# A two-direction Mamba-2 block with a feed-forward layer: all instruction orders drawn anew, a transpose of 64 columns in place of 32, and an unread negation taken out

## Chip, cores and metric

One core of a Trainium2 chip. The metric is the device time of one execution in microseconds (us), the median of several runs.

## What is computed

Eight sequences of 512 tokens, 256 wide, all float32. Each is layer-normed and goes through two Mamba-2 blocks, one forward in time and one backward (d = 0 and d = 1 below); their outputs are projected and added to the input, then comes a second layer norm and a linear layer with a low-rank correction.

```python
zxbcdt = x @ Win                       # 256 -> 2*512 + 2*64 + 8
z, xBC, dt = split(zxbcdt)
xBC = silu(causal_conv4(xBC) + convb)
xs, Bm, Cm = split(xBC)                # 8 heads of 64, state of 64
dt = softplus(dt + dtb); dA = exp(dt * -exp(Alog))
h = dA_t * h + dt_t * B_t x_t;  y_t = C_t h          # over 512 tokens
y = (y + Dsk * xs) * silu(z)
y = y * rsqrt(mean(y*y) + 1e-5) * normw
out_d = y @ Wout
x = x + concat(out_fwd, out_rev) @ Wo + bo
x = x + layernorm(x) @ W.T + b + (layernorm(x) @ V_r) @ C.T
```

## The kernel before

The scan is done in four chunks of 128 tokens, with matmuls inside a chunk and a carried state between chunks. All work of a sequence is cut into steps, and each engine (TensorE `pe`, ScalarE `act`, VectorE `dve`, GpSimd `pool`, and SyncE `sp`, which issues the DMAs) has a list of step calls written out by hand in a fixed order. Semaphores tie the lists together. An engine works its list strictly in order, so a step that waits holds up all that stands behind it on its engine.

The stages in time are `opening` (weights split into a high and a low part, the output weights folded into one, first projections), `first_scan` (sequence 0 forward), then a loop of six passes and the same two lists once more behind it: `reversed_scan` (the backward scan of sequence b, with the projections of sequence b+1 for the forward direction) and `forward_scan` (the forward scan of b+1, with the projections for its backward direction and the second layer norm and feed-forward of sequence b). `last_scan` is the backward scan of the last sequence and the end.

The steps that matter here, with the lines of the profile:

- TensorE. `project(b, d, t)` (L488 to L490): one of nine tiles of 128 output channels, 6 matmuls of 512 columns, into the ring `pj` of three PSUM banks; tile 0 holds B and C, tiles 1 to 4 the values xs, tiles 5 to 8 the gate z. `b_tokens` (L539) and `x_tokens` (L548): transposes of B and xs. `norm_transposed` (L472), `scores` (L555, into `gm`), `squares` (L608), `sums` (L526, L527), `mix` (L622, output projection, a quarter of the tokens each), `norm2_transposed` (L681), `feed` (L688), `dt_project` (L508, L509), `dt_transposed` (L518, 32 rows). `state` (L568) and `intra` (L581) write 64 rows of PSUM with two matmuls side by side; `inter` (L599) uses quarters of 64 by 64; `s_transposed` (L533) transposes the running sums. Everything with `mi` in the profile shares a ring of two PSUM banks; its turns are the lists `START`, `LOOP` and `LAST`.
- ScalarE. `conv_start` (L936) takes a projected tile out of PSUM with the first convolution tap, `conv_end` (L945) applies Silu to the finished tile, `gate` (L950) applies Silu to z. `bound` (L969, Relu, four instructions) and `decay` (L975, Exp) turn the repeated running sums into decay weights, one head each, h = 0 to 7; `decay_w` (L954) and `decay_e` (L959) are Exp on small tiles. `row_copy` (L922) and `row_decays` (L927, Exp) put the transposed sums into the rows that are sent to DRAM and back. `soft_exp` (L914) and `soft_log` (L918, Ln) belong to the softplus. `square` (L989), `norm1_scale` (L998), `norm2_scale` (L1003) and `norm2` (L1008) need no table of their own.
- VectorE. `conv` (L1409, three taps a tile), `weights` (L1436, decay times scores), `x_tokens` (L1421), `state` (L1446, L1448), `outputs` (L1455), `mix` (L1476), `norm2_bn` (L1487), `norm1_aggr` (L1321) and `norm2_aggr` (L1492), `s_copy` (L1383: sums out of PSUM), `s_neg` (L1391: writes `neg_s`, which nothing reads) and `s_rest` (L1397: writes `wd`).
- GpSimd. `decayed_x` (L1907), `decayed_c` (L1913), `decayed_state` (L1921), `gate` (L1928), `add_square` (L1936), and the small steps of the norms (L1852 to L1888).
- SyncE. `put_rows` and `put_decays` write the rows to DRAM, `repeat_heads` (L336) and `repeat_decays` bring them back spread over all partitions, `copy_c` copies C.

x_tokens(j = 0) waits for the four conv_end of its direction, intra(p) for the weights of its two heads, inter(0) for the state of the third chunk on VectorE, mix(0) for all four gated tiles.

```python
            def s_transposed(phase, it, b, d):
                released(phase, it, f"{d}S")
                ps, full = misc(phase, it, f"{d}ST")
                alone(pe)
                pe.transpose(ps[0:NCH, 0:Q], s_all[:, d, 0].rearrange("p c h -> p (c h)"), ident).then_inc(full, 1)
```

NCH is 32, Q is 128; `s_all[:, d]` holds the 32 running sums and then the 32 sums at the chunk ends.

Of the kernel before, what the change touches and what calls it, by code (L numbers as in the profile page):

```python
# [23 lines left out]
ALU = mybir.AluOpType  # L24
ACT = mybir.ActivationFunctionType

P = 128
# [26 lines left out]
START = (["a0", "a1", "dtm", "dtt", "w0", "w1", "w2", "w3", "w4", "0S", "w5", "w6", "0ST", "w7", "w8"]  # L54
         + ["0bt", "0x0", "0x1", "0s0", "0x2", "0x3", "1S", "1ST", "0s1", "0s2"])
LOOP = ["1bt", "1x0", "1x1", "1x2", "1x3", "a0", "a1", "1s0", "1s1", "dtm", "dtt", "0ss", "0o0", "1s2",
        "0o1", "0S", "0ST", "0bt", "0x0", "0x1", "0x2", "0x3", "0s0", "1ss", "0s1", "0s2", "1o0", "1o1",
        "1S", "1ST", "t0", "t1", "f0", "f1", "t2", "t3", "f2", "f3"]
LAST = ["1x0", "1bt", "1x1", "1x2", "1s0", "1x3", "1s1", "0ss", "1s2", "0o0", "0o1", "1o0", "1o1"]
# [15 lines left out]
def build(nc, x, consts, selcol, win, convw, convb, dtb, alog, dskip, normw, woutT, wo, bo, ffT, ffb, vrT, cT, out):  # L75
    with ExitStack() as ctx:
# [57 lines left out]
        neg_s = sb("neg_s", [P, 2, NCH])  # L134
# [45 lines left out]
        def ring(name, n=2):  # L180
# [8 lines left out]
         r_ready, al_ready, s_ready, wd_ready, w_ready, conv_first,  # L189
# [5 lines left out]
            "r_ready al_ready s_ready wd_ready w_ready conv_first bc_ready "  # L195
# [50 lines left out]
        def _(sp):  # L246
# [110 lines left out]
            def opening():  # L357
                load_first(0)
                load_first(1)
                load_first(2)  # L360
                load_first(3)
                load_consts()
                load_small(0)
                load_win(0, 0, 0)
                load_small(1)
                load_win(0, 0, 1)
                load_fold(0)
                load_win(0, 1, 0)
                load_dt()
                load_fold(1)  # L370
                load_fold(2)
                load_win(0, 1, 1)
                load_rest()
# [3 lines left out]
                load_win(1, 1, 1)  # L377
                copy_c(0, 0)
                load_x("start", 0, 1)
                put_rows("start", 0, 0, 0)  # L380
                repeat_heads(0, 0, 0)
                put_decays(0, 0)
                repeat_heads(0, 0, 1)
                repeat_decays(0, 0, 0)
                repeat_decays(0, 0, 1)
                repeat_heads(0, 0, 2)
                repeat_heads(0, 0, 3)
                load_residual0()
                put_rows("start", 0, 0, 1)
                repeat_decays(0, 0, 2)  # L390
                repeat_decays(0, 0, 3)
                repeat_heads(0, 1, 0)
                put_decays(0, 1)
                copy_c(0, 1)
                repeat_decays(0, 1, 0)
                repeat_heads(0, 1, 1)
# [6 lines left out]
            def turn(it, more):  # L403
# [6 lines left out]
                repeat_heads(it + 1, 0, 1)  # L410
                repeat_heads(it + 1, 0, 2)
                repeat_decays(it + 1, 0, 0)
# [5 lines left out]
                store("loop", it, it, 0)  # L418
# [3 lines left out]
                put_decays(it + 1, 1)  # L422
                store("loop", it, it, 1)
                repeat_heads(it + 1, 1, 1)
                repeat_decays(it + 1, 1, 0)
                repeat_decays(it + 1, 1, 1)
                store("loop", it, it, 2)
# [17 lines left out]
        def _(pe):  # L445
# [432 lines left out]
        def _(act):  # L878
# [1269 lines left out]
```

## Time and profile before

| | |
|---|---|
| median of 3 runs | 633.09 us (632.95 to 633.33) |
| the profiled execution: time, span | 633.48 us, 631.6 us |
| mean granted TensorE clock | 0.989 of full speed |
| TensorE matmul busy | 598.1 us |
| ScalarE busy | 551.9 us |
| VectorE busy | 477.6 us |
| GpSimd busy | 349.4 us |

The span is from the first to the last instruction of the profiled execution; its time is the device time of that same execution. Busy times overlap between engines. A share of busy time is an average over stages, so what an engine's work is worth is read in its stage.

### The profile page before, as it was taken

Reading aid. Unit: us, or ns where it says so; the run is one execution under the profiler, and the core shown is the slowest. Engines: PE = TensorE matmul, PEld = TensorE weight load, DVE = VectorE, ACT = ScalarE, POOL = GpSimd, SP = SyncE. Lnnn points to the kernel's source line nnn. Section 1 sums busy time; section 2 is a strip of 40 time slices with the busy share of each in tenths; the row PEclk is TensorE's granted clock in tenths of the full one; section 3 lists DMA queues with packets and bytes.
Section 4 is the critical chain, followed back from the end, with each engine's and each line's share of the span. In section 5 each row is a group of like instructions: output and inputs, shape, how many; then the busy total and the mean of one; then the engine's idle time right before and its main releaser. Section 6 shows DMA issues by size and latency. Waiting matters only on the chain.

```text
span 631.6 us, 14046 instructions
## 1 busy us (share of the span) xinstructions
PE 598.1 (95%) x4380; PEld 472.2 (75%) x4380; DVE 477.6 (76%) x1007; ACT 551.9 (87%) x1236; POOL 349.4 (55%) x367
## 2 busy tenths in 40 slices
PE   1997999999999999999999999999999999999896
PEld 1675678877888777877788777877778778787674
DVE  3679677985979779786879869796788869687453
ACT  3699999979998999979999899989999799988932
POOL 1015746577464854757375764748446673748713
PEclk9999999999999999999999999999999999999896
DMA  7533703327260541507232361505424171515400
GB/s 220 149 127 117 238 22 117 88 75 204 57 179 5 163 146 50 160 11 259 64 122 63 111 198 25 185 1 186 122 77 133 50 226 27 149 38 145 135 1 33
DMA packets 43545, 70.71 MB, mean 112 GB/s; under 512 B 8000, under 2 KB 30592, under 8 KB 43520
## 3 DMA queue, kind: packets, MB, share of 16 engines
q1 hardware_dynamic: 43520, 70.40, 37.2%
q8 instruction: 13, 0.21, 0.2%
q14 instruction: 12, 0.10, 0.0%
HBM read 59.37 MB, written 4.72 MB: 101 GB/s over the span
## 4 chain that ended last, share of the span: by engine, by line
PE 82%; DVE 5%; ACT 4%; POOL 3%; issue 2%; DMA 1%; SPq 1%; POOLq 0%; DVEq 0%
PE mi L622 18%; PE pj L488 10%; PE pj L490 9%; PE pj L489 9%; PE py L581 8%; PE py L599 4%; PE mi L688 4%; PE mi L568 4%; PE mi L548 3%; PE gm L555 2%; PE mi L608 2%; PE mi L681 2%; DVE xdt L1421 2%; ACT bs L969 1%; PE mi L472 1%
## 5 line engine op out<-in xcount | busy, mean ns | idle before, releaser
L1409 DVE SCALAR_TENSOR_TENSOR xc<-pj,cw,xc 128x510 f32<-128x510 f32 (+2 forms) x240 | 173.9, 738 | 13.7 <-ACT xc L936 12.8
L969 ACT ACTIVATE bs<-bs,s_all 128x128 f32<-128x128 f32 x512 | 161.1, 388 | 0.0
L488 PE MATMUL pj<-xnt_hi,w_hi 128*128 128x512 f32 x288 | 122.0, 424 | 4.1 <-DVE xnt_lo L1326 3.4
L1928 POOL TENSOR_TENSOR yg<-yg,sz 128x512 f32<-128x512 f32 x60 | 76.7, 1284 | 86.0 <-DVE yg L1455 85.5
L490 PE MATMUL pj<-xnt_hi,w_lo 128*128 128x512 f32 x288 | 114.5, 398 | 0.0
L622 PE MATMUL mi<-wc,yg 128*128 128x256 f32 x480 | 114.2, 389 | 0.3 <-DVE ss L1468 0.3
L489 PE MATMUL pj<-xnt_lo,w_hi 128*128 128x512 f32 x288 | 114.4, 397 | 0.0
L622 PEld LDWEIGHTS mi<-wc,yg 128*128 128x128 f32 x480 | 89.4, 191 | 16.1 <-issue 4.7
L1436 DVE TENSOR_TENSOR bs<-bs,gm 128x512 f32<-128x512 f32 x128 | 85.1, 680 | 10.6 <-ACT bs L975 10.6
L936 ACT ACTIVATE xc<-pj,cb,cw 128x512 f32<-128x512 f32 x80 | 60.7, 767 | 31.9 <-PE pj L490 31.7
L975 ACT ACTIVATE bs<-bs 128x512 f32<-128x512 f32 x128 | 78.6, 622 | 1.5
L1421 DVE TENSOR_TENSOR xdt<-mi,dt 128x512 f32<-128x512 f32 x64 | 43.3, 686 | 42.6 <-PE mi L548 42.1
L1907 POOL TENSOR_TENSOR xw<-xdt,w_end 128x512 f32<-128x512 f32 x48 | 49.2, 1045 | 46.1 <-ACT w_end L954 42.7
L488 PEld LDWEIGHTS pj<-xnt_hi,w_hi 128*128 128x128 f32 x288 | 54.7, 190 | 26.6 <-issue 10.1
L1936 POOL TENSOR_TENSOR sqsum<-sqsum,sq 128x512 f32<-128x512 f32 x45 | 57.8, 1285 | 29.1 <-ACT sq L989 28.3
L581 PE MATMUL py<-bs,xdt 128*64 128x128 f32 x1024 | 69.4, 278 | 0.7 <-DVE bs L1436 0.5
L581 PEld LDWEIGHTS py<-bs,xdt 128*64 128x64 f32 x1024 | 56.2, 137 | 16.9 <-issue 8.1
L1913 POOL TENSOR_TENSOR es<-cc,es 128x384 f32<-128x384 f32 x64 | 64.2, 1009 | 4.0 <-DMA es<-rows_dram 3.9
L490 PEld LDWEIGHTS pj<-xnt_hi,w_lo 128*128 128x128 f32 x288 | 54.7, 190 | 12.8
L489 PEld LDWEIGHTS pj<-xnt_lo,w_hi 128*128 128x128 f32 x288 | 54.9, 191 | 10.0
L1455 DVE SCALAR_TENSOR_TENSOR yg<-xs,dsk,py 128x512 f32<-128x512 f32 x64 | 46.6, 738 | 4.7 <-PE py L599 4.7
L548 PE MATMUL mi<-cst,xs 128*128 128x128 f32 x256 | 38.4, 278 | 1.7 <-ACT xs L945 0.3
(150 smaller groups left out, 968.2 us busy)
## 6 DMA issues: line engine op xcount, KB each, us to landing
bs<-rows_dram SPq DMA_DIRECT2D x64, 512.0 KB, 5.0
es<-rows_dram SPq DMA_DIRECT2D x128, 96.0 KB, 4.1
cc<-bcm SPq DMA_DIRECT2D x32, 128.0 KB, 2.5
xres<-in_x SPq DMA_DIRECT2D x8, 512.0 KB, 3.9
out<-ot SPq DMA_DIRECT2D x32, 128.0 KB, 1.9
xin<-in_x SPq DMA_DIRECT2D x7, 512.0 KB, 4.4
cz<-bcm SPq DMA_DIRECT2D x16, 128.0 KB, 3.1
rows_dram<-s_rows SPq DMA_DIRECT2D x128, 4.0 KB
```

Source lines behind the costliest of these rows:

```text
L488: pe.matmul(ps[:], hi(k), xnt_hi[:, k, :], start=(k == 0), stop=False)
L489: pe.matmul(ps[:], hi(k), xnt_lo[:, k, :], start=False, stop=False)
L490: mm = pe.matmul(ps[:], lo(k), xnt_hi[:, k, :], start=False, stop=(k == KD - 1))
L581: pe.matmul(py[bank][HP * half:HP * half + HP, Q * c:Q * c + Q], xdt[:, c, HP * h:HP * h + HP], bs[:, h, Q * c:Q * c + Q], start=(c == 0), ...
L622: mm = pe.matmul(ps[:, D * i:D * i + D], yg[:, d, t, Q * c:Q * c + Q], wc[:, d, t, :], start=(t == 0), stop=(t == KI - 1))
L936: nc.scalar.activation(xc[:, t, :], pj[bank][:], ACT.Identity, bias=cb[:, d, t:t + 1], scale=cw[:, d, t, KW - 1:KW]).then_inc(conv_first, 1)
L969: i = nc.scalar.activation(bs[:, h, Q * c:Q * c + Q], bs[:, h, Q * c:Q * c + Q], ACT.Relu, bias=s_all[:, d, 0, c, h:h + 1], scale=-1.0)
L975: nc.scalar.activation(bs[:, h, :], bs[:, h, :], ACT.Exp, scale=-1.0).then_inc(decayed, 1)
L1409: i = dve.scalar_tensor_tensor(xc[:, t, to], pj[bank][:, of], cw[:, d, t, KW - 1 - s:KW - s], xc[:, t, to], ALU.mult, ALU.add)
L1436: dve.tensor_tensor(bs[:, h, :], bs[:, h, :], gm[:], ALU.mult).then_inc(m_ready, 1)
L1913: pool.tensor_tensor(es[:, p, LATER[d]], cc[:, d, LATER[d]], es[:, p, LATER[d]], ALU.mult).then_inc(c2_ready, 1)
L1928: pool.tensor_tensor(yg[:, d, p, :], yg[:, d, p, :], sz[:, d, p, :], ALU.mult).then_inc(yg_ready, 1)
```

## The change

1. Every list of steps of every engine is written in another order, and with them the turns of the `mi` ring. Below are the two loop lists of TensorE and the reversed one of ScalarE, and parts of the others.
2. `s_transposed` takes 64 columns (both halves of `s_all[:, d]`) and writes 64 rows; `row_copy` reads the first 32 as before.
3. `s_neg` and `neg_s` are gone; `bound` waits for `wd_ready` in place of `s_ready`.
4. GpSimd's `decayed_c` waits for `cc_loaded` at its first pair.

```diff
-                pe.transpose(ps[0:NCH, 0:Q], s_all[:, d, 0].rearrange("p c h -> p (c h)"), ident).then_inc(full, 1)
+                pe.transpose(ps[0:2 * NCH, 0:Q], s_all[:, d].rearrange("p s c h -> p (s c h)"), ident).then_inc(full, 1)
...
                 if h == 0:
-                    act.wait_ge(s_ready, u + 1)
+                    act.wait_ge(wd_ready, u + 1)
...
             def decayed_c(b, d, p):
 
+                if p == 0:
+                    pool.wait_ge(cc_loaded[d], 48 * (b + 1))
```

TensorE, `reversed_scan`:

```diff
+                b_tokens(phase, it, b, 1)
                 project(b, 1, NT - 1)
-                b_tokens(phase, it, b, 1)
                 x_tokens(phase, it, b, 1, 0)
...
                 state(phase, it, b, 1, 0)
+                wait_xnt(phase, it)
+                dt_project(phase, it)
+                project(nxt, 0, 0)
+                project(nxt, 0, 1)
                 state(phase, it, b, 1, 1)
-                wait_xnt(phase, it)
-                project(nxt, 0, 0)
-                dt_project(phase, it)
-                project(nxt, 0, 1)
+                dt_transposed(phase, it)
                 project(nxt, 0, 2)
-                dt_transposed(phase, it)
                 squares(phase, it, b, 0)
                 mix(phase, it, b, 0, 0)
                 mix(phase, it, b, 0, 1)
+                state(phase, it, b, 1, 2)
                 intra(b, 1, 0)
-                state(phase, it, b, 1, 2)
                 intra(b, 1, 1)
+                inter(phase, it, b, 1, 0)
                 project(nxt, 0, 3)
                 mix(phase, it, b, 0, 2)
-                inter(phase, it, b, 1, 0)
                 mix(phase, it, b, 0, 3)
                 sums(phase, it, nxt, 0)
+                project(nxt, 0, 4)
+                s_transposed(phase, it, nxt, 0)
                 intra(b, 1, 2)
-                project(nxt, 0, 4)
                 intra(b, 1, 3)
-                s_transposed(phase, it, nxt, 0)
                 inter(phase, it, b, 1, 1)
```

TensorE, `forward_scan` (after the first six steps; in these x_tokens 0 and b_tokens change places):

```diff
                 x_tokens(phase, it, b, 0, 3)
+                project(b, 1, 1)
+                squares(phase, it, last, 1)
                 state(phase, it, b, 0, 0)
-                project(b, 1, 1)
+                state(phase, it, b, 0, 1)
                 project(b, 1, 2)
-                squares(phase, it, last, 1)
-                state(phase, it, b, 0, 1)
+                mix(phase, it, last, 1, 0)
+                mix(phase, it, last, 1, 1)
                 state(phase, it, b, 0, 2)
                 intra(b, 0, 0)
-                mix(phase, it, last, 1, 0)
-                mix(phase, it, last, 1, 1)
                 intra(b, 0, 1)
                 inter(phase, it, b, 0, 0)
                 mix(phase, it, last, 1, 2)
                 mix(phase, it, last, 1, 3)
+                project(b, 1, 3)
                 sums(phase, it, b, 1)
-                project(b, 1, 3)
                 project(b, 1, 4)
                 s_transposed(phase, it, b, 1)
                 intra(b, 0, 2)
+                intra(b, 0, 3)
                 norm2_transposed(phase, it, last, 0)
-                intra(b, 0, 3)
                 norm2_transposed(phase, it, last, 1)
...
                 norm2_transposed(phase, it, last, 3)
+                project(b, 1, 5)
+                project(b, 1, 6)
                 feed(phase, it, 2)
                 feed(phase, it, 3)
-                project(b, 1, 5)
-                project(b, 1, 6)
                 project(b, 1, 7)
```

ScalarE, `reversed_scan`, from its middle:

```diff
                 decay(b, 1, 5)
                 soft_log(nxt)
+                conv_start(nxt, 0, 2)
                 conv_end(nxt, 0, 0)
-                conv_end(nxt, 0, 1)
                 bound(b, 1, 6)
-                decay(b, 1, 6)
                 conv_start(nxt, 0, 3)
                 bound(b, 1, 7)
+                decay(b, 1, 6)
                 decay(b, 1, 7)
+                conv_end(nxt, 0, 1)
+                row_copy(phase, it, 0)
                 conv_start(nxt, 0, 4)
                 square(phase, it, b, 1, 0)
-                row_copy(phase, it, 0)
+                row_decays(phase, it, 0)
                 square(phase, it, b, 1, 1)
-                row_decays(phase, it, 0)
                 conv_end(nxt, 0, 2)
+                gate(nxt, 0, 5)
                 conv_end(nxt, 0, 3)
-                gate(nxt, 0, 5)
-                conv_end(nxt, 0, 4)
                 gate(nxt, 0, 6)
                 square(phase, it, b, 1, 2)
+                conv_end(nxt, 0, 4)
                 gate(nxt, 0, 7)
                 square(phase, it, b, 1, 3)
```

ScalarE's `forward_scan` is changed in the same manner: bound and its decay stand apart (bound 1, bound 2, conv_start 0, decay 1, ...), row_decays stands directly behind row_copy, norm2_scale 2 ahead of norm2 0. In `last_scan` gate(b, 1, 8) moves from behind decay 7 to between decay 1 and decay 2. VectorE's `forward_scan` has conv(b, 1, 2, 1) ahead of state 2, weights 5 ahead of mix 2, and

```diff
                 norm2_bn(phase, it, last, 3)
+                if ahead:
+                    norm1_aggr(b + 1, 2)
                 norm2_aggr(last, 0)
+                if ahead:
+                    norm1_aggr(b + 1, 3)
                 norm2_aggr(last, 1)
                 norm2_aggr(last, 2)
+                s_copy(phase, it, 1)
                 norm2_aggr(last, 3)
                 conv(b, 1, 2, 2)
-                s_copy(phase, it, 1)
```

GpSimd's has norm1_neg between norm2_var and norm2_root, and norm1_var between norm2_root and norm2_shift. SyncE's `opening` loads the dt weights and the first projection weights ahead of the constants and small vectors, and has repeat_decays(0, 0, 2) and (0, 0, 3) ahead of put_rows of the second direction.

## Rows read from the trace of the kernel before

**Rows 1.** The page, sections 1 and 4: busy time of all engines, and the chain.
```profile
PE 598.1 (95%) x4380; PEld 472.2 (75%) x4380; DVE 477.6 (76%) x1007; ACT 551.9 (87%) x1236; POOL 349.4 (55%) x367
...
PE 82%; DVE 5%; ACT 4%; POOL 3%; issue 2%; DMA 1%; SPq 1%; POOLq 0%; DVEq 0%
```

**Rows 2.** Busy time by stretch: one pass, then its reversed and forward scan.
```profile
core 0: us, PE busy (x) PEld busy (x) DVE busy (x) ACT busy (x) POOL busy (x), PEclk, DMA share, GB/s
221.04:294.15 73.11, 72.33 (x543) 57.58 (x543) 58.55 (x124) 67.53 (x154) 44.39 (x47) 1.00 0.37 113
218.22:254.07 35.85, 35.34 (x265) 27.41 (x264) 28.09 (x58) 34.05 (x76) 19.41 (x20) 1.00 0.35 106
254.07:291.32 37.25, 36.98 (x280) 30.16 (x279) 30.46 (x65) 33.48 (x78) 24.98 (x28) 1.00 0.39 113
```

**Rows 3.** TensorE's timeline (start us, duration us, engine, line, operation); last row: the chain.
```profile
162.78 0.60 PE L568 MATMUL mi<-xw,btok 128*64 128x256 f32 x4
163.21 1.04 PE L581 MATMUL py<-bs,xdt 128*64 128x128 f32 x16
...
258.10 0.60 PE L548 MATMUL mi<-cst,xs 128*128 128x128 f32 x4
258.62 0.65 PE L568 MATMUL mi<-xw,btok 128*64 128x256 f32 x4
259.21 0.50 PE L488 MATMUL pj<-xnt_hi,w_hi 128*128 128x512 f32 x1
...
261.63 0.39 PE L489 MATMUL pj<-xnt_lo,w_hi 128*128 128x512 f32 x1
261.86 0.40 PE L490 MATMUL pj<-xnt_hi,w_lo 128*128 128x512 f32 x1
262.10 0.95 PE L608 MATMUL mi<-cst,sqsum 128*128 128x1 f32 x8
...
109.77 0.87 PE mi L548 x8
```

**Rows 4.** TensorE's timeline, forward scan, from the last project pass to the feeds.
```profile
276.92 0.40 PE L490 MATMUL pj<-xnt_hi,w_lo 128*128 128x512 f32 x1
277.16 0.28 PE L533 MATMUL mi<-cst,s_all 128*32 128x128 f32 x1
277.39 1.09 PE L581 MATMUL py<-bs,xdt 128*64 128x128 f32 x16
278.75 0.44 PE L681 MATMUL mi<-cst,xn 128*128 128x128 f32 x2 [0.27 <-ACT xn L1003]
...
282.15 0.38 PE L681 MATMUL mi<-cst,xn 128*128 128x128 f32 x2
```

**Rows 5.** Groups of ScalarE's instructions by form: table loads (count, busy us, mean ns).
```profile
L945 ACT ACT_TABLE_LOAD x24 | 30.8, 1283 | 0.4
...
L954 ACT ACT_TABLE_LOAD x16 | 20.5, 1283 | 0.3
...
L918 ACT ACT_TABLE_LOAD x8 | 10.3, 1283 | 0.1
...
L975 ACT ACT_TABLE_LOAD x7 | 9.0, 1283 | 0.1
```

**Rows 6.** ScalarE's timeline, reversed scan: conv_start 4 with its wait, and conv_end 4.
```profile
246.44 0.78 ACT L936 ACTIVATE xc<-pj,cb,cw 128x512 f32<-128x512 f32 x1 [1.12 <-PE pj L490]
...
251.51 0.62 ACT L945 ACTIVATE xs<-xc 128x512 f32<-128x512 f32 x1
```

**Rows 7.** ScalarE's timeline, forward scan: norm2_scale 0 and 1, and the second norm2.
```profile
278.10 1.09 ACT L1003 ACTIVATE xn<-xres,shift,rstd 128x256 f32<-128x256 f32 x2 [0.17 <-POOL shift L1888]
...
280.62 0.38 ACT L1008 ACTIVATE xn2t<-mi 128x256 f32<-128x256 f32 x1
```

**Rows 8.** Timelines of VectorE (four norm2_aggr) and GpSimd (norm1_neg), forward scan.
```profile
275.56 0.41 DVE L1492 BATCH_NORM_AGGREGATE mv<-st 128x2 f32<-128x6 f32 x4
...
278.07 0.23 POOL L1865 TENSOR_SCALAR negm<-mv 128x4 f32<-128x4 f32 x1
```

**Rows 9.** GpSimd's timeline in the first scan: the wait for the repeated decays.
```profile
64.49 1.02 POOL L1913 TENSOR_TENSOR es<-cc,es 128x384 f32<-128x384 f32 x1 [3.51 <-DMA es<-rows_dram]
```

More of the change, by code:

```diff
@@ L422, in turn @@
                 put_decays(it + 1, 1)
+                store("loop", it, it, 0)
                 store("loop", it, it, 1)
@@ L759, in last_scan @@
                 phase, it, b = "last", 0, NB - 1
+                project(b, 1, NT - 1)
+                b_tokens(phase, it, b, 1)
+                scores(phase, it, b, 1)
                 x_tokens(phase, it, b, 1, 0)
-                b_tokens(phase, it, b, 1)
-                project(b, 1, NT - 1)
                 x_tokens(phase, it, b, 1, 1)
@@ L1604, in first_scan @@
+                x_tokens(phase, it, 0, 1)
+                conv(b, 1, 1, 2)
+                x_tokens(phase, it, 0, 2)
                 norm1_bn(b + 1, 3)
-                conv(b, 1, 0, 1)
-                x_tokens(phase, it, 0, 1)
+                s_copy(phase, it, 1)
+                norm1_aggr(b + 1, 0)
+                scores(b, 0)
                 state(phase, it, b, 0, 0)
-                conv(b, 1, 0, 2)
-                x_tokens(phase, it, 0, 2)
-                norm1_aggr(b + 1, 0)
-                conv(b, 1, 1, 1)
@@ L1612, in first_scan @@
-                dt_floor(b, 1)
-                scores(b, 0)
+                s_rest(phase, it, 1)
+                conv(b, 1, 1, 3)
+                x_tokens(phase, it, 0, 3)
                 norm1_aggr(b + 1, 1)
-                x_tokens(phase, it, 0, 3)
-                s_copy(phase, it, 1)
+                norm1_aggr(b + 1, 2)
                 weights(phase, it, b, 0, 0)
-                conv(b, 1, 0, 3)
-                conv(b, 1, 1, 2)
-                norm1_aggr(b + 1, 2)
-                s_neg(phase, it, 1)
@@ L1717, in forward_scan @@
+                if ahead:
                     norm1_bn(b + 1, 3)
-                dt_decay(b, 1)
-                weights(phase, it, b, 0, 1)
-                squares(phase, it, 1)
+                conv(b, 1, 0, 2)
+                conv(b, 1, 0, 3)
+                weights(phase, it, b, 0, 2)
+                weights(phase, it, b, 0, 3)
                 if ahead:
                     norm1_aggr(b + 1, 0)
-                state(phase, it, b, 0, 1)
-                weights(phase, it, b, 0, 2)
+                conv(b, 1, 1, 1)
@@ L1725, in forward_scan @@
+                conv(b, 1, 2, 1)
+                mix(phase, it, last, 1, 0)
                 if ahead:
                     norm1_aggr(b + 1, 1)
-                conv(b, 1, 0, 2)
-                conv(b, 1, 1, 1)
-                weights(phase, it, b, 0, 3)
+                state(phase, it, b, 0, 2)
+                mix(phase, it, last, 1, 1)
+                weights(phase, it, b, 0, 4)
                 conv(b, 1, 1, 2)
-                state(phase, it, b, 0, 2)
+                norm2_bn(phase, it, last, 0)
@@ L1732, in forward_scan @@
                 dt_floor(b, 1)
-                conv(b, 1, 0, 3)
-                mix(phase, it, last, 1, 0)
-                mix(phase, it, last, 1, 1)
-                conv(b, 1, 2, 1)
-                if ahead:
-                    norm1_aggr(b + 1, 2)
-                weights(phase, it, b, 0, 4)
+                outputs(b, 0, 0)
+                norm2_bn(phase, it, last, 1)
                 conv(b, 1, 1, 3)
-                norm2_bn(phase, it, last, 0)
-                if ahead:
-                    norm1_aggr(b + 1, 3)
```

432 lines of the change are left out of this document (214 added, 218 removed).

## The prediction

> **What bounds the kernel now.** I read the page first. TensorE is busy for 95% of the span, ScalarE for 87%, and the chain that ended last runs through TensorE for 82% [rows 1]. The busy time of each engine by stretch comes next. One pass of the loop takes 73.1 us, and seven such passes follow each other: six of the loop and one written out behind it. In a pass TensorE is busy 72.3, ScalarE 67.5, VectorE 58.6 and GpSimd 44.4 us. The pass has two stretches, each from its first x_tokens or b_tokens transpose on TensorE: the reversed scan of 35.85 us, where ScalarE is busy 34.05 and idle 1.80, and the forward scan of 37.25 us, where it is busy 33.48 and idle 3.77 [rows 2]. So TensorE leads, and ScalarE is right behind it, in the reversed scan above all. The timelines of both engines then give the prices of the two things that the new orders change: TensorE's changes of tile shape, and ScalarE's table loads.
>
> **TensorE's changes of tile shape.** project, x_tokens, scores, squares, mix, sums and feed run at 128\*128, state and intra at 128\*64, inter at 64\*64, dt_transposed at 32\*128, s_transposed at 128\*32. In the old order a pass has 14 changes of shape in each scan. In the new one I count 11 in the reversed scan (state 0 | dt_project, two projects | state 1 | dt_transposed | ... mix | state 2, intra 0, 1 | inter | ... | s_transposed, intra 2, 3 | inter | project) and 9 in the forward scan: 8 fewer in a pass. The price is read where one state stands alone between transposes and projects [rows 3]. From the transposes at 258.10 to the squares at 262.10 are 4.00 us. The same work without a change: 4 transposes at 0.109 (8 took 0.87) are 0.44, one state is 0.43 (162.78 to 163.21, intra behind it at the same shape), 12 project passes at 0.23 are 2.79; together 3.66. Two changes cost 0.34 us, 0.17 each. The Trainium skill ("TensorEngine Tiling (Array Packing)", Key Properties) says that changing the tiling mode drains the engine; by that rule, the trace agrees.
>
> Eight changes at 0.17 are 1.36 us in a pass. One pair was cheaper: in the forward scan s_transposed starts 0.24 behind the last project pass, as another pass would, and intra follows 0.23 behind it [rows 4]; less the 0.11 of a transpose, its two changes cost 0.12 together, and its new form, one change into 128\*64, costs about as much. I take 1.2 us in a pass, 8.4 in seven, all of it on TensorE's own queue. The wider transpose (64 columns for 32) sends the same 128 columns through, with double the weight columns, whose load lies beside other work; its rows 32 to 63 in PSUM are read by nobody. I cost it at nothing; if the load were exposed, 16 loads of under 0.1 us each are the bound.
>
> **ScalarE's table loads.** Exp, Ln and Silu each need a table load of 1.283 us in front when another of them ran before; Relu, Identity, Copy and Square have none in the loop [rows 5]. Of these 24 + 16 + 8 + 7 = 55 loads, 49 are the loop's, 7 in each pass, and 6 stand at the ends. The new reversed scan puts one conv_end (Silu) behind decay 6 and 7 (Exp) and ahead of row_decays (Exp), which now stands before square 1 and conv_end 2 (Silu). The sequence was Exp, Ln, Silu, Exp, Silu, and is now Exp, Ln, Silu, Exp, Silu, Exp, Silu: two loads more, 2.57 us in a pass, 18.0 in seven. The forward scan keeps its two. The last scan puts a Silu gate among the decays: one more.
> The Trainium skill ("ScalarE: Activation LUTs", What ACT_TABLE_LOAD costs) gives about 2.7 us for a load. By that figure the addition would be some 38 us instead of 18.0; this case's rows show 1.283, and the sum goes by them.
>
> The 2.57 us don't fit into the 1.80 us that ScalarE is idle in the reversed scan [rows 2]. There I follow ScalarE. conv_end 4 started 33.29 us into that scan (251.51 less 218.22), with one wait of 1.12 us before it [rows 6]. The new order adds 2.57 of loads, moves gate 6 and square 2 ahead of it (about 0.5 each, by the steps of the rows, 1.0), and has work in place of the wait: 33.29 + 2.57 + 1.0 - 1.12 = 35.74. It takes 0.62, so x_tokens of the forward scan, which reads its result, can start at 36.4, less about 0.1 that bound and its own decay gain by standing apart: 36.3. TensorE alone, with 0.5 us of changes saved, would be there at 35.3. The reversed scan comes out 0.4 us longer, and its whole gain on TensorE is spent in front of that wait.
>
> **The forward scan.** The second layer norm decides it: mix 2 and 3 on TensorE, then statistics on VectorE, four small steps on GpSimd, norm2_scale and norm2 on ScalarE, then norm2_transposed and feed. It bound before: TensorE sat idle 0.27 us at 278.75 for norm2_scale [rows 4]. Mix 3 ends 0.3 earlier (two changes fewer ahead of it), but state 2 on VectorE now stands behind conv(1, 2, 1), which waits for ScalarE, and inter 0 waits for that state: I give 0.25 back. Behind the mixes, VectorE gets norm1_aggr 2 and 3 and s_copy among the norm2 statistics: four aggregates took 0.41 us [rows 8], so 0.3 for these. GpSimd gets norm1_neg and norm1_var among its four steps, each 0.2 [rows 8], 0.35 with their issue. norm2_scale starts 0.6 later than before. Intra 3, which used to stand between the first two transposes and covered ScalarE's copy, now stands ahead of them. From the first scale to the end of the second copy ScalarE takes 2.9 us (278.10 to 281.00) [rows 7], and the second feed ends about 0.9 behind that: 278.70 + 2.9 + 0.9 = 282.5 where it was 282.15 [rows 4]. The forward scan comes out 0.3 us longer, and its 0.7 of changes and 0.3 of idle time are gone into the wait for norm2.
>
> **The rest.** neg_s is read by nobody; bound now waits for wd, whose step stands where the negation stood, so it costs nothing, and VectorE has 14 us idle in a pass to cover it. GpSimd's decayed_c waits for the copy of C, which scores on TensorE wait for anyway. On SP's queue the repeats of the decays move ahead of put_rows in the start, where GpSimd stood 3.51 us waiting for es [rows 9]; with the earlier weight loads I take 1.0 us off, between 0 and that wait. The stores and repeats of the loop change places, with the copies early enough in both. The last scan has 6 changes of shape fewer, 1.0 us; its extra 1.28 us table load I take as hidden in ScalarE's waits there, and it is the bound on the other side.
>
> **Sum.** Seven passes of 0.4 + 0.3 are +4.9; start and end -2.0. The profiled execution took 633.48 us (span 631.6), so 636.4; it lies 0.4 above the median of 633.09, against which the forecast is 636.0.
>
> **Rivals.**
> 1. TensorE keeps the lead, faster (chance 0.28). Then the saved changes come out whole, -8.4, and start and end give -2.0: 622.7; with half of it lost to waits, 628. For it: 72.3 of 73.1 us busy. Against it: ScalarE's 67.5 + 2.57 = 70.1 us in a pass of 71.9 would leave 1.8 us idle, and its waits for project 3 and for norm2 in the forward scan alone were more. It decides where conv_end 4 ends less than 35.3 us into the reversed scan.
> 2. Both even out (0.16): the ScalarE chain is 0.4 us shorter in each pass than I make it, and the time is 633, within 0.2%, about what a measurement of this kernel can tell from no change.
> 3. The waits add up (0.13): the state of VectorE, norm2 and ScalarE's tail each come out on their long side, 1.0 to 1.3 us in a pass: 640 to 642.
> 4. The change does not do what it says: the 64-column transpose does not share intra's shape, or the table loads are not placed as I count them. The first costs 0.17 a scan, 2.4 us; the second is rival 1. It has no chance of its own beyond 0.01, taken with rival 3.
>
> The forecast itself, 634.4 to 640, has 0.43. Slower by over 0.2%: 0.43 + 0.13 = 0.56; within 0.2%: 0.16; faster: 0.28. The range leaves out a tenth on each side: down to 625.0, into rival 1, and up to 641.0.
>
> **What would show it.** ACT_TABLE_LOAD counts of 9 in a pass, about 70 at the lines that had 55; ScalarE busy about 570 us in all. TensorE's idle time in front of x_tokens at the forward scan's start, released by ScalarE's conv_end, some 0.7 us a pass, and in front of feed, released by norm2. State alone between projects less often, each remaining change still about 0.17. Passes of 73.8 us. It is wrong if passes are under 72.5, if ScalarE's loads stay at 7, or if x_tokens finds its input ready.

## The result and the profile after

The changed kernel takes 641.29 us (median of 4 runs, 639.2 to 643.15), the kernel before 633.02 beside it: ratio 1.0133, 95% interval 1.0106 to 1.016. It is slower by 8.3 us, where +2.9 was forecast; the range ended at 641.0. The profiled execution took 639.2 us with a span of 637.2. It was the fastest of the four, so the two traces lie only 5.7 us apart.

The page of the kernel after, busy time and the chain that ended last; it answers to [rows 1]:

```profile
PE 592.8 (93%) x4380; PEld 468.5 (74%) x4380; DVE 471.3 (74%) x991; ACT 568.4 (89%) x1251; POOL 347.3 (55%) x367
...
ACT 45%; PE 21%; DVE 15%; issue 12%; POOL 6%; DVEq 0%; ACTq 0%; DMA 0%; SPq 0%; POOLq 0%
```

TensorE works 5.3 us less than before and ScalarE 16.5 us more, and the chain now runs through ScalarE (45% for 4%) and only for 21% through TensorE (82% before). Two cautions. A part of TensorE's 5.3 us is the clock, as the last section shows. And the chain's shares alone don't show who causes a loss: kernels 6 and 7 below differ by 1 us, and TensorE's share of the chain is 75% in one and 23% in the other.

Busy time of one pass by stretch, of the kernel after, and its reversed and forward scan, each from the first x_tokens; it answers to [rows 2]:

```profile
221.12:295.62 74.50, 72.03 (x543) 57.14 (x542) 57.62 (x121) 69.74 (x154) 44.11 (x47) 1.00 0.36 110
221.12:257.57 36.45, 34.97 (x265) 27.01 (x263) 27.17 (x56) 35.97 (x75) 20.35 (x20) 1.00 0.37 109
257.57:295.62 38.05, 37.07 (x279) 30.13 (x280) 30.45 (x65) 33.77 (x80) 23.76 (x28) 1.00 0.36 111
```

A pass is 1.4 us longer than before: 0.60 in the reversed scan and 0.80 in the forward scan. In the reversed scan TensorE is idle for 1.48 us and ScalarE for only 0.48. Of the 1.48, 0.95 are two waits for ScalarE, shown below; the other 0.53 are waits for VectorE among the x_tokens, which cost nothing new, since the four x_tokens take 2.82 us in both kernels.

ScalarE's table loads by form, after (count, busy us, mean ns):

```profile
L944 ACT ACT_TABLE_LOAD x30 | 38.5, 1283 | 0.5
L953 ACT ACT_TABLE_LOAD x16 | 20.5, 1283 | 0.3
L917 ACT ACT_TABLE_LOAD x8 | 10.3, 1283 | 0.1
L926 ACT ACT_TABLE_LOAD x8 | 10.3, 1283 | 0.1
L974 ACT ACT_TABLE_LOAD x8 | 10.3, 1283 | 0.1
```

With the two at the gate and one at norm1_scale they are 73, where 58 were: 14 of the 15 more are two in each of seven passes, at conv_end (L944) and at row_decays (L926), which had none of its own in the loop. The fifteenth is the one in the last scan.

TensorE's timeline, after, at the end of the reversed scan (in brackets the idle time and who ended it):

```profile
255.52 0.50 PE L487 MATMUL pj<-xnt_hi,w_hi 128*128 128x512 f32 x1 [0.57 <-ACT sz L949]
...
257.57 0.66 PE L547 MATMUL mi<-cst,xs 128*128 128x128 f32 x4 [0.38 <-ACT xs L944]
```

and ScalarE's, same stretch:

```profile
247.63 1.28 ACT L944 ACT_TABLE_LOAD   x1
248.93 0.63 ACT L944 ACTIVATE xs<-xc 128x512 f32<-128x512 f32 x1
...
250.92 1.28 ACT L926 ACT_TABLE_LOAD   x1
252.21 0.31 ACT L926 ACTIVATE s_rows<-s_rows 32x128 f32<-32x128 f32 x1
252.43 0.62 ACT L988 ACTIVATE sq<-yg 128x512 f32<-128x512 f32 x1
253.06 1.28 ACT L944 ACT_TABLE_LOAD   x1
...
256.89 0.63 ACT L944 ACTIVATE xs<-xc 128x512 f32<-128x512 f32 x1
```

Between 247.63 and 254.34 ScalarE loads three tables (Silu, Exp, Silu) where it loaded one. conv_end 4 starts 35.77 us into the scan; TensorE's project 7 waits 0.57 us for the gate to give back a bank (that wait was not in the forecast), then x_tokens 0.38 for conv_end 4.

### The profile page after: what moved, and what is told of

Same layout as the page of the kernel before. It is cut to its first block, busy times and chain, and to the rows that moved or that the text cites. A ratio compares the mean times of both kernels' runs of the same rounds, so it can differ in the third digit from the quotient of the medians.

```text
span 637.2 us, 14055 instructions
## 1 busy us (share of the span) xinstructions
PE 592.8 (93%) x4380; PEld 468.5 (74%) x4380; DVE 471.3 (74%) x991; ACT 568.4 (89%) x1251; POOL 347.3 (55%) x367
## 4 chain that ended last, share of the span: by engine, by line
ACT 45%; PE 21%; DVE 15%; issue 12%; POOL 6%; DVEq 0%; ACTq 0%; DMA 0%; SPq 0%; POOLq 0%
ACT bs L968 14%; ACT bs L974 5%; PE mi L687 4%; DVE xc L1405 4%; PE pj L487 3%; ACT xc L935 3%; PE pj L488 3%; PE pj L489 3%; ACT L953 3%; DVE bs L1432 2%; ACT sz L949 2%; ACT L944 2%; ACT sq L988 2%; DVE yg L1451 2%; POOL yg L1922 2%
## 5 line engine op out<-in xcount | busy, mean ns | idle before, releaser
L487 PE MATMUL pj<-xnt_hi,w_hi 128*128 128x512 f32 x288 | 125.4, 435 | 5.3 <-ACT sz L949 3.9
L621 PE MATMUL mi<-wc,yg 128*128 128x256 f32 x480 | 110.0, 382 | 0.0
L974 ACT ACTIVATE bs<-bs 128x512 f32<-128x512 f32 x128 | 76.4, 621 | 0.7
L580 PE MATMUL py<-bs,xdt 128*64 128x128 f32 x1024 | 64.8, 277 | 0.9 <-DVE yg L1451 0.3
L547 PE MATMUL mi<-cst,xs 128*128 128x128 f32 x256 | 37.0, 278 | 6.7 <-DVE xdt L1417 3.5
```

The lines of the kernel that those rows point to most:

```text
L487: pe.matmul(ps[:], hi(k), xnt_hi[:, k, :], start=(k == 0), stop=False)
L580: pe.matmul(py[bank][HP * half:HP * half + HP, Q * c:Q * c + Q], xdt[:, c, HP * h:HP * h + HP], bs[:, h, Q * c:Q * c + Q], start=(c == 0), ...
L621: mm = pe.matmul(ps[:, D * i:D * i + D], yg[:, d, t, Q * c:Q * c + Q], wc[:, d, t, :], start=(t == 0), stop=(t == KI - 1))
L974: nc.scalar.activation(bs[:, h, :], bs[:, h, :], ACT.Exp, scale=-1.0).then_inc(decayed, 1)
```

## The experiments

The numbers are those of the labels; there was no run 3. Each ran in 5 rounds beside the kernel before, whose median in them was 631.8 to 632.8 us, so ratios to it compare better across experiments than medians do. Passes are lengths from x_tokens to x_tokens in the third pass of each trace; by that measure the scans of before are 36.3 and 36.8 us, since b_tokens (0.43 us) there stands ahead of x_tokens and falls into the reversed scan.

**1. The two loads out of the changed kernel.** ScalarE, `reversed_scan`:

```diff
                 decay(b, 1, 7)
-                conv_end(nxt, 0, 1)
...
                 square(phase, it, b, 1, 1)
+                conv_end(nxt, 0, 1)
                 conv_end(nxt, 0, 2)
```

> The changed kernel (641.3 us), with one step of ScalarE moved: in reversed_scan conv_end(nxt, 0, 1) goes from behind decay 7 to behind square(b, 1, 1), so that row_decays (Exp) follows the decays without a Silu between. Theory A (the table loads set the reversed scan): ACT_TABLE_LOAD falls by 14, the two waits of TensorE for ScalarE's gate 5 and conv_end 4 (0.57 and 0.38 us in the pass I read) go, a pass of 74.5 us falls to 73.3 to 73.6 because the forward scan, which is held by the second layer norm, keeps its 38.1 us; 632 to 635 us in all. Theory B (the loads lie beside other work, and the loss is in the orders of TensorE, VectorE and GpSimd): a pass stays above 74.2 us and the time above 639 us.

Measured: 629.57 us (628.28 to 630.83), ratio 0.9951 [0.9933, 0.997]. One step moved turns 8 us of loss into 3 us of gain, 2.4 us better than the near end of what was expected. The pass of this kernel, by stretch as above:

```profile
218.09:252.96 34.87, 34.33 (x264) 27.36 (x263) 27.09 (x56) 33.63 (x73) 20.12 (x20) 1.00 0.42 119
252.96:290.93 37.97, 37.02 (x280) 30.11 (x280) 29.45 (x65) 33.68 (x80) 24.14 (x28) 1.00 0.38 111
```

The reversed scan falls from 36.45 to 34.87, and ScalarE's busy time in it by 2.34. ScalarE's timeline of the same kernel shows that it now even waits:

```profile
251.65 0.63 ACT L988 ACTIVATE sq<-yg 128x512 f32<-128x512 f32 x1 [0.68 <-POOL yg L1922]
252.19 0.61 ACT L944 ACTIVATE xs<-xc 128x512 f32<-128x512 f32 x1
```

and TensorE goes from project into x_tokens without idle time. The loads cost 1.58 us a pass in the reversed scan and 0.08 in the forward one, 11.7 us in all: more than the whole loss.

**2. The same two loads put into the kernel before.** ScalarE, `reversed_scan`: conv_end(nxt, 0, 1) moved from behind conv_end(nxt, 0, 0) to behind decay(b, 1, 7), all else as before.

> The kernel before (633.0 us), with conv_end(nxt, 0, 1) moved behind decay 7 in ScalarE's reversed_scan, which puts the same two table loads a pass (2.57 us) into the old orders. Theory A: ScalarE had 1.8 us idle in the reversed scan, so most is absorbed there; 0.8 us over and a ScalarE that reaches the forward scan 1.4 us later cost 0.2 to 0.8 us a pass, 634.5 to 638.5 us. Theory B: within 0.5 us of 633.0.

Measured: 637.65 us (636.12 to 638.64), ratio 1.0079 [1.0058, 1.01]. The pass, by stretch:

```profile
220.30:257.25 36.95, 36.08 (x270) 27.75 (x269) 28.08 (x58) 36.51 (x78) 19.53 (x20) 1.00 0.37 109
257.25:294.31 37.06, 36.80 (x277) 29.65 (x276) 30.34 (x65) 33.41 (x79) 24.84 (x28) 1.00 0.40 115
```

Here the same 2.57 us of ScalarE cost 0.9 us in each of six passes and 0.6 in the seventh, 5.9 in the trace and 5.0 by the ratio. That a load costs more in the new orders (1.66 us a pass) fits with TensorE being ready sooner there, so that it waits for ScalarE longer; no run takes this reason apart further.

**5. The old loop, with the new start and end, and 4. the old loop and the old end.** In 5, `LOOP`, `reversed_scan` and `forward_scan` of all engines are those of before, the 64-column transpose and the missing negation stay. In 4, `LAST` and `last_scan` are old as well.

> The changed kernel with the loop's orders of before on every engine (reversed_scan, forward_scan, the loop list of the mi ring, SyncE's turn); opening, first_scan and last_scan, the 64-column transpose and the missing negation stay new. From the two traces: the seven passes lost 11.6 us, the start gained 0.5 and the last scan about 5.4. If those add up, 627 to 628 us, 6 below the kernel before. If the last scan's gain came only from how the new loop hands over to it, 632 to 633.

> As the one before, with last_scan's old orders too: only opening, first_scan, the 64-column transpose and the missing negation are new. Expected 0.5 us below the kernel before, 632.0 to 633.0. If the 64 columns or the missing negation matter for the loop (16 transposes; the negation once took 1.3 us on VectorE), it shows here as more than 1 us either way.

Measured: 5 gives 631.82 us (630.83 to 633.12), ratio 0.9985 [0.9971, 1.0]; 4 gives 633.5 us (632.0 to 634.71), ratio 1.0016 [1.0002, 1.003]. Their passes are 73.13 us, against 73.11 before [rows 2]: the transpose and the negation do nothing in the loop. The new start costs 1.0 us (4), and the new end takes 1.7 off (5 against 4). Of the 1.7 a part is the clock: executions of 4 and 5 with the same granted clock (0.995 or 0.997) lie only 0.6 to 0.8 us apart.

The 5.4 us that the last scan was expected to give were no gain of that size. Between the two traces it shrank from 49.05 to 43.54 us. 2.2 us of this only move in front of the mark, since the new last scan starts its x_tokens later (the seventh pass is 71.8 us long in kernel 4 and 74.0 in kernel 5). And with all its orders old, kernel 4's last scan takes 46.89: TensorE ran at half clock for 6.8 us of it, for 13.6 us in the kernel before.

The start's trace says why the forecast gain didn't come. TensorE's first x_tokens, in the kernel before and, in the second fence, in kernel 4:

```profile
43.04 0.60 PE L548 MATMUL mi<-cst,xs 128*128 128x128 f32 x4
```

```profile
46.17 0.60 PE L547 MATMUL mi<-cst,xs 128*128 128x128 f32 x4
```

The first scan is 2.3 us shorter (26.7 for 28.96 us), and GpSimd's 3.51 us wait for the repeated decays [rows 9] is gone, but the opening in front of it is 3.1 us longer. In the eleven traces with the new opening the first x_tokens start at 44.9 to 46.3 us, in the four with the old one at 42.6 to 43.3; the changed kernel's own trace, with 44.86, is the shortest of the eleven. The trace also shows where the time goes first. The new list of SyncE loads the dt weights ahead of the last quarter of x, and VectorE's statistics wait for that quarter; the first matmul follows. Kernel 4, then the kernel before:

```profile
5.47 0.43 DVE L1315 BATCH_NORM_STATS2 st<-xin 128x6 f32<-128x256 f32 x1 [1.23 <-DMA xin<-in_x]
11.21 1.94 PE L471 MATMUL mi<-cst,xin 128*128 128x128 f32 x8 [11.21 <-ACT xin L997]
```

```profile
9.52 1.94 PE L472 MATMUL mi<-cst,xin 128*128 128x128 f32 x8 [9.52 <-ACT xin L998]
```

The first project, now behind dt_project, starts at 17.70 us for 14.84. No run takes the pieces of the opening apart.

**10 and 11. Each new scan with the other scan old.** 10: the reversed scan of experiment 1 with the forward scan of before. 11: the reversed scan of before with the new forward scan.

> The changed kernel with the two table loads taken out of its reversed scan as in the first experiment, and with the forward scan of before on TensorE, ScalarE, VectorE and GpSimd (and its turns of the ring). Theory, the forward loss is the new forward order's own: reversed scan 34.9 us as in the first experiment, forward scan 36.8 as before, a pass of 71.7, and 7 x 1.15 less than the 629.57 of that experiment: 621.5 us. Rival, what the reversed scan gains is lost in the forward scan whichever order that has (ScalarE, busy for 67.5 of a pass, or a transfer holds it): the forward scan grows to about 38, the pass stays at 72.8, the time at 629.5.

> The changed kernel with the reversed scan of before (no table load added) and its own new forward scan. Theory, the forward loss is the new forward order's own: reversed 36.3, forward 38.0, a pass of 74.3, and with the 631.8 us of the new start and end around the old loop, 7 x 1.15 more: 640 us, as long as the changed kernel though no table load is added. Rival, the forward scan was only late because the new reversed scan left its work late: forward 36.8, 632 us.

Measured: 10 gives 626.33 us (626.13 to 628.26), ratio 0.9912 [0.9894, 0.9931]; 11 gives 634.84 us (633.05 to 636.97), ratio 1.0041 [1.0024, 1.0058]. The forward scans, of 10 and then of 11:

```profile
252.28:289.19 36.91, 36.65 (x277) 29.68 (x276) 30.24 (x64) 33.27 (x79) 24.55 (x28) 1.00 0.36 108
```

```profile
256.33:294.15 37.82, 36.91 (x280) 30.20 (x279) 30.28 (x65) 33.23 (x78) 23.99 (x28) 1.00 0.39 120
```

Both misses, of 5 us, are of size: b_tokens moves its 0.43 us from one scan to the other, and I had added lengths from kernels with the two placings, which is most of the 0.5 to 0.6 us a pass that the forecasts were off. The whole passes don't suffer from that:

| pass, us | old forward | new forward |
|---|---|---|
| old reversed | 73.13 (kernel 5) | 73.68 (11) |
| new reversed, loads out | 72.21 (10) | 72.84 (1) |
| new reversed, with loads | not run | 74.50 (after) |

The new reversed order gains 0.9, the new forward order loses 0.6, and the two loads lose 1.7. That the forward order loses by itself, with no load added, is shown by 11: its interval lies wholly above that of kernel 5, which has the old loop.

**6. norm2's chain cleared.** Experiment 1, and norm1_aggr 2 and 3 and s_copy behind the four norm2_aggr on VectorE, norm1_neg and norm1_var behind norm2_shift on GpSimd:

```diff
                 norm2_bn(phase, it, last, 3)
-                if ahead:
-                    norm1_aggr(b + 1, 2)
                 norm2_aggr(last, 0)
-                if ahead:
-                    norm1_aggr(b + 1, 3)
                 norm2_aggr(last, 1)
                 norm2_aggr(last, 2)
-                s_copy(phase, it, 1)
                 norm2_aggr(last, 3)
+                if ahead:
+                    norm1_aggr(b + 1, 2)
+                    norm1_aggr(b + 1, 3)
+                s_copy(phase, it, 1)
```

> The kernel of e1_two_loads_out (629.6 us, pass 72.86: reversed 34.87, forward 37.97), with the second layer norm first in the forward scan: on VectorE norm1_aggr 2 and 3 and s_copy go behind the four norm2_aggr, on GpSimd norm1_neg and norm1_var go behind norm2_shift. If the norm2 chain sets the forward scan, as I forecast with 0.65 us for these two insertions, norm2_scale starts 0.5 to 0.65 us earlier and so does all behind it: a pass of 72.2 to 72.4, 625 to 627 us. Rival: TensorE waits there for intra's weights or for feed's results anyway, or s_copy now arrives late and holds s_transposed: 629 us or more.

Measured: 626.33 us (626.13 to 628.38), ratio 0.9907 [0.9886, 0.9929]. Its forward scan:

```profile
252.06:289.45 37.39, 36.82 (x280) 30.16 (x280) 30.61 (x65) 33.77 (x80) 24.14 (x28) 1.00 0.36 111
```

0.58 us less than in experiment 1. Five small steps of 0.1 to 0.3 us each, put among others, cost the forward order nearly all that it loses; they were moved together, so what each one costs isn't shown.

**7. intra 3 between the transposes again.** Kernel 6, and on TensorE intra(b, 0, 3) back between norm2_transposed 0 and 1, which adds two changes of tile shape.

> The one before, with intra(b, 0, 3) on TensorE back between norm2_transposed 0 and 1: two changes of tile shape more, but intra covers ScalarE's norm2_scale 1 and 2 and norm2 0. If the missing cover costs what I forecast (TensorE idle 0.27 + 0.34 us ahead of the transposes and 0.34 ahead of feed in that place), a pass gains up to 0.5 us net of 0.34 for the changes: 0.2 to 0.5 us a pass below e6, 1.4 to 3.5 us. If the changes cost more than the cover brings, it is 0 to 2 us slower than e6.

Measured: 625.29 us (624.64 to 627.01), ratio 0.9893 [0.9869, 0.9916]; the pass is 0.08 us shorter, where 0.2 to 0.5 was expected. By the times alone (both intervals overlap) it is no difference. So the cover that the step gives for ScalarE's copy is worth at least two changes of shape; TensorE's own steps (its timeline summed from start to start, each wait put at what the same pair of steps takes without one) come to 36.64 us in both forward scans, so no price of these two changes is to be seen.

**12. 32 columns again.** Kernel 7 with the transpose as before the change, nothing moved.

> The seventh kernel (two loads out, norm2 first, intra 3 between the transposes; 625.29 us) with the transpose of the running sums at 32 columns again, nothing moved: in each scan 128*128, 128*32, 128*64 in place of 128*128, 128*64, one change of tile shape more, 14 in seven passes. Theory of the prediction, 0.17 us for a change: +2.4 us, 627.7, and in a pass 0.34. Rival, a change costs only the 0.05 to 0.1 us between two starts that the timeline shows there: +0.7 to 1.4, 626 to 626.7. Rival, it hides behind the waits for norm2: 625.3.

Measured: 625.88 us (624.39 to 627.34), ratio 0.9898 [0.9878, 0.9918], no difference; passes 72.16 us for 72.19. TensorE's timeline around the place, of kernel 7 and then of 12:

```profile
275.94 0.28 PE L532 MATMUL mi<-cst,s_all 128*64 128x128 f32 x1
276.14 1.09 PE L580 MATMUL py<-bs,xdt 128*64 128x128 f32 x16
277.59 0.44 PE L680 MATMUL mi<-cst,xn 128*128 128x128 f32 x2 [0.35 <-ACT xn L1002]
```

```profile
275.35 0.27 PE L532 MATMUL mi<-cst,s_all 128*32 128x128 f32 x1
275.55 1.10 PE L580 MATMUL py<-bs,xdt 128*64 128x128 f32 x16
277.01 0.44 PE L680 MATMUL mi<-cst,xn 128*128 128x128 f32 x2 [0.36 <-ACT xn L1002]
```

intra starts 0.20 us behind the transpose with the shape changed and with it unchanged, so this change has no price; a wait of 0.35 us for ScalarE stands behind it that would hide one in the pass, but not between these two starts. The reversed scan, where no such wait follows, is 34.87 us long for 34.88: no price there either. The Trainium skill ("TensorEngine Tiling (Array Packing)", Key Properties) says that changing the tiling mode drains the engine; at this place no time for a drain is to be seen.

**8 and 9. Two changes of shape fewer, and two more, by one moved step.** In the kernel before, 8 moves state 0 of the forward scan to directly in front of state 1; 9 moves squares between state 1 and state 2; each with its turn of the ring.

```diff
                 x_tokens(phase, it, b, 0, 3)
-                state(phase, it, b, 0, 0)
                 project(b, 1, 1)
                 project(b, 1, 2)
                 squares(phase, it, last, 1)
+                state(phase, it, b, 0, 0)
                 state(phase, it, b, 0, 1)
```

> The kernel before (632.5 us, pass 73.11), with state(b, 0, 0) on TensorE's forward scan moved from in front of project(b, 1, 1) to right in front of state(b, 0, 1), behind squares, and the mi ring's list to match: two changes of shape fewer, nothing else. At 0.17 us a change, with TensorE the bound, 0.34 us a pass: 630.1. If TensorE's saved time turns into a wait further on (ScalarE, norm2), the pass moves by less than 0.1 us.

> The kernel before, with squares on TensorE's forward scan moved from in front of state(b, 0, 1) to between state(b, 0, 1) and state(b, 0, 2), and the mi ring's list to match: two changes of shape more, nothing else. At 0.17 us a change 0.34 us a pass, 634.9 us. If TensorE had slack there, less than 0.1 us a pass.

Measured: 8 gives 647.02 us (646.54 to 651.73), ratio 1.0252 [1.0219, 1.0285]; 9 gives 645.52 us (642.82 to 645.84), ratio 1.0195 [1.0169, 1.0221]. Both missed by more than 10 us, and neither time measures a change of shape. Kernel 8 on VectorE, then on TensorE:

```profile
268.30 0.42 DVE L1446 COPY hst<-mi 128x256 f32<-128x256 f32 x1 [1.43 <-PE mi L568]
```

```profile
270.29 1.08 PE L568 MATMUL mi<-xw,btok 128*64 128x256 f32 x8 [2.04 <-DVE ss L1468]
```

The moved state is late for VectorE, which stands behind it for 1.43 us with all its later work, and TensorE then stands 2.04 us for a bank that VectorE gives back late. In 9 the same goes through the ring of two banks: TensorE waits 0.87 us in front of state 2 for VectorE's state 1. The passes are 75.0 us long in kernel 8 and 74.4 in 9, for 73.1; two passes of 9 are 76.0, and in each of these two the granted clock was at half for 3.4 us.

The trace of kernel 8 does hold the price that the prediction read in [rows 3], since the state is gone from between these transposes and squares and no wait stands among them:

```profile
263.49 0.60 PE L548 MATMUL mi<-cst,xs 128*128 128x128 f32 x4
...
266.72 0.95 PE L608 MATMUL mi<-cst,sqsum 128*128 128x1 f32 x8
```

That is 3.23 us, for 4.00 with the state in between. A state takes 0.43 beside another, so 0.34 are left: a state that stands alone costs what the prediction said. Whether its change of tile shape or its change of work is the cause isn't told apart by this; in 12, where the shape alone changes, the price is nothing.

**13 and 14. The rest of the forward loss.** 13: kernel 7 with weights 5 behind s_copy in place of ahead of mix 2. 14: 13 with VectorE's state 2 ahead of conv(1, 2, 1).

> The seventh kernel (625.29 us, pass 72.20) with VectorE's weights 5 moved from in front of mix 2 to behind the copy of the running sums, where it stood before the change. In the changed kernel's trace VectorE takes mix 2 0.43 us behind the start of TensorE's next project, against 0.20 in the kernel before (where it was idle for 0.60 us in front of it), since weights 5 of 0.69 us lies between. Theory, that is the rest of the forward scan's loss: 0.2 us a pass, 1.4 us less, 623.9, forward scan 37.1. Rival, norm2 no longer sets the forward scan after the two earlier repairs: no difference, 625.3. Rival, weights 5 is now late for decay 5 and intra 2: slower, up to 0.3 us a pass, 627.4.

> The kernel of the run beside it (weights 5 later) with VectorE's state 2 also moved ahead of conv(1, 2, 1). In the seventh kernel inter 0 waits 0.17 us on TensorE for that state, and mix 2 and 3 stand behind inter 0. Theory, mix 2 and 3 and with them norm2 come 0.17 us earlier in each pass: 1.2 us less than the kernel beside it, 622.7. Rival, norm2 is held by GpSimd's own steps and ScalarE, not by mix 3: 623.9, no difference to it.

Measured: 13 gives 625.36 us (623.42 to 627.38), ratio 0.99 [0.9867, 0.9933], a pass 0.06 us shorter than in 7: no difference. 14 gives 624.73 us (622.35 to 625.32), ratio 0.9876 [0.9845, 0.9906]; the two intervals overlap widely, but the pass is 0.23 us shorter, and all middle passes of the loop agree in it: 71.9. Forward scans of 13 and of 14:

```profile
252.01:289.27 37.26, 36.74 (x280) 30.07 (x280) 30.81 (x65) 33.73 (x80) 24.10 (x28) 1.00 0.38 113
```

```profile
252.16:289.19 37.03, 36.67 (x280) 30.01 (x280) 29.87 (x65) 33.77 (x80) 24.21 (x28) 1.00 0.36 110
```

My reading of weights 5 was wrong: with it gone VectorE is idle for 0.47 us in front of mix 2, so it had filled a wait. VectorE's late state 2 was the other part. Kernel 14 is the fastest of all, by the ratios 1.2% below the kernel before and 2.5% below the changed one.

## Why the prediction was wrong

The direction and the mechanism held, the size didn't: +8.3 us against +2.9. Step by step:

- **The table loads: right.** 9 in a pass, 73 in all, 1.283 us each; ScalarE busy 568.4 against "about 570". Taking two out freed 2.34 us of ScalarE in the scan of experiment 1. The Trainium skill ("ScalarE: Activation LUTs", What ACT_TABLE_LOAD costs) gives 1.283 us for the load itself, as measured here, and adds 1.38 us of drain, 2.66 in all for a switch; the two would have freed 5.3 by that, an estimate from the page. This trace has no room for such a drain: the Silu behind the load of 247.63 starts at 248.93. The measurement decides.
- **The reversed scan: nearly right, by two errors that met.** conv_end 4 was forecast 35.74 us into the scan and started at 35.77; x_tokens at 36.3 and came at 36.45, after the wait for ScalarE that was named. But "TensorE alone, with 0.5 us of changes saved, would be there at 35.3" was wrong: it is there at 34.87 (experiment 1). In the reversed scan three changes of shape fewer were priced at 0.5 us; the scan without the loads is 1.0 shorter (35.85 to 34.87), and so is TensorE's busy time (35.34 in [rows 2] to 34.33). What gives the other 0.5 isn't shown. So the loads cost 1.58 us in this scan, not the 1.0 that the step implies; and without them the new orders are faster than the old, as rival 1 had it.
- **The forward scan: the step that failed.** Forecast +0.3, measured +0.80. "norm2_scale starts 0.6 later than before": it starts 1.10 later. Measured from the start of each scan, term by term: VectorE takes mix 2 0.21 later (20.25 for 20.04 us), where "mix 3 ends 0.3 earlier ... I give 0.25 back" made 0.05 earlier; from there to GpSimd's first step 2.51 us for 2.06, +0.45 where 0.3 was priced; GpSimd's steps to norm2_scale 2.37 for 1.93, +0.44 where 0.35 was. The timeline of GpSimd, after, against [rows 8]:

```profile
280.33 0.23 POOL L1873 TENSOR_SCALAR negm<-mv 128x4 f32<-128x4 f32 x1 [2.33 <-DVE mv L1488]
280.62 0.19 POOL L1844 TENSOR_SCALAR ve<-mv 128x4 f32<-128x4 f32 x1
280.89 0.22 POOL L1857 TENSOR_SCALAR negm<-mv 128x4 f32<-128x4 f32 x1
281.08 1.04 POOL L1848 TENSOR_TENSOR rstd<-ve,halves 128x4 f32<-128x4 f32 x1
282.20 0.19 POOL L1844 TENSOR_SCALAR ve<-mv 128x4 f32<-128x4 f32 x1
282.47 0.20 POOL L1880 TENSOR_TENSOR shift<-negm,rstd 128x4 f32<-128x4 f32 x1
```

  The third and fifth rows are norm1's, put among norm2's. VectorE's three steps cost more than their engine time since norm1_aggr and s_copy break a group of four that took 0.41 in one piece. The "0.7 of changes" that this scan was to save isn't there either: TensorE's own steps, summed as in experiment 7, come out only about 0.2 us shorter, with five changes fewer. Its waits come out 1.0 longer: in front of inter 0, for norm2_scale (0.25 and 0.13) and in front of feed. TensorE's timeline, after:

```profile
273.21 0.89 PE L598 MATMUL py<-es,hst 64*64 64x128 f32 x24 [0.18 <-DVE hst L1444]
...
283.36 1.00 PE L680 MATMUL mi<-cst,xn 128*128 128x128 f32 x4 [0.25 <-ACT xn L1002]
284.70 1.97 PE L687 MATMUL mi<-wff,xn2t 128*128 128x256 f32 x8 [0.34 <-ACT xn2t L1007]
```

  The first feeds end 28.93 us into the scan (286.50), where 28.4 was forecast and 28.08 was before.
- **The ends: half right.** Last scan -1.7 by the medians and -0.6 to -0.8 at equal clock (forecast -1.0), start +1.0 (forecast -1.0): the wait for the repeated decays went as forecast, but the new opening is longer, and I had costed only the part of it that gained. "The earlier weight loads" were booked as part of the gain; one of them stands ahead of the last load of x and holds up the first matmul.
- **No cost for the transpose and the negation: right** (73.13 for 73.11 us a pass). The 64 columns save nothing either: the two changes at this place, priced at 0.12 us, are no part of what the reversed scan gains.
- **The sum.** The loop gave 7 times 1.40, +9.8, where 4.9 was forecast; start and end together give -1.0 by ratio (kernel 5) where -2.0 was forecast. +8.8 stands against +8.3 measured; the ratios of the changed kernel and of kernel 5 give 9.4 for the loop. Rival 3 (waits add up, 1.0 to 1.3 us a pass, 640 to 642 us, chance 0.13) is what happened, at its upper side; a chance of 0.13 was too little with four short chains in a row, each priced at its bare engine time.

**What stays open.** What a change of tile shape costs by itself: none to be seen in experiments 12 and 7, but 0.17 for each side of a state that stands alone, in [rows 3] and again in kernel 8. The 0.17 may belong to the change of work and not of shape. So 0.17 for every change was too general a price. Also open are the other 0.5 us of the reversed scan and how much of the opening's loss each moved load causes.

## What to carry to other kernels

Count table loads before anything else when an activation engine's list is reordered: here two loads a pass cost a third of what they take beside the old orders and two thirds beside the new, faster ones, and one moved step makes or removes them. Small steps put into a chain of latencies between engines cost more than their busy time, even when each engine is idle for a fifth of the pass and more. A step moved to save the leader's own time must first be checked for who takes its result: in experiment 8 a step moved by 3.6 us for two changes of shape cost 14.

## What the runs showed that was not expected

In the last scan TensorE's granted clock drops to half for some microseconds, and not for the same time in every execution. Stretches of the kernel before (the clock is the third number from the right):

```profile
593.20:596.60 3.40, 3.40 (x13) 2.33 (x13) 0.91 (x2) 3.37 (x11) 3.40 (x5) 0.50 0.11 38
606.90:617.10 10.20, 9.69 (x84) 8.06 (x83) 3.50 (x6) 1.36 (x3) 4.06 (x3) 1.00 0.01 2
617.10:627.30 10.20, 6.92 (x20) 4.67 (x19) 5.11 (x18) 3.40 (x8) 4.24 (x7) 0.50 0.04 13
```

and of the kernel after:

```profile
598.80:602.20 3.40, 3.40 (x25) 2.32 (x26) 1.80 (x4) 3.35 (x7) 2.79 (x5) 0.51 0.95 264
629.60:633.00 3.40, 3.33 (x11) 2.63 (x11) 0.85 (x2) 1.36 (x4) 1.95 (x2) 0.50 0.11 39
```

The half level is 1.2 GHz of 2.4. In the kernel before, 13.6 us of the last scan ran at it, in the one after 6.8; in front of the long one TensorE had been busy for 9.69 of 10.20 us at the full level. In these two traces all passes of the loop ran at 1.00. Single executions of the kernel before lay between 630.81 and 634.95 us in 25 runs, and they sort by the granted clock: 634.9 on average at 0.987 (4 runs), 632.7 at 0.989 (14), 631.7 at 0.995 (5), 630.9 at 0.997 (2). So the length of the last scan in one profile says little. Changes of a few microseconds are better read from the middle passes of the loop, the second to the sixth, which agree within 0.05 us in each trace whose loop ran at the full level, as here in 12, 13 and 14; the first and the seventh also carry what the new start and end shift.
